# One loop for TensorE over both layers, a bias table with its heads side by side, and products that nobody reads

## The reference

```
x = x + attention(group_norm(x))          # twice

def attention(x):                          # windows of 8 x 8 tokens, shifted by 4; 16 heads of 16
    q, k, v = xw @ Wq.T, xw @ Wk.T, xw @ Wv.T + bv
    logits = norm(q) @ norm(k).T * exp(min(logit_scale, log 100))
    tab = relu(table @ cpb_w1.T + cpb_b1) @ cpb_w2.T       # 225 positions x 16 heads
    logits += 16 * sigmoid(tab[relative position])          # 64 x 64 x 16
    logits = where(mask, -inf, logits)
    z = softmax(logits) @ v @ Wo.T + bo
```

## Time and profile before

| | |
|---|---|
| median of three runs | 826.88 us (823.43 to 829.28) |
| the profiled execution | 830.89 us, its span 828.7 us |
| mean granted clock of TensorE | 0.933 of full speed |
| busy: TensorE, its weight loads | 750.0 us, 670.4 us |
| busy: VectorE, ScalarE, GpSimd | 530.2, 519.3, 556.1 us |

### The profile page before, as it was taken

One profiled execution on the slowest core, in us unless ns is written; L12 is line 12 of the kernel. 1 busy time (PEld: TensorE's weight loads), 2 busy tenths in 40 slices (PEclk: granted clock), 3 DMA queues, 4 the chain that ended last, 5 costly groups with the idle time before them and its releaser, 6 DMA issues.

```text
span 828.7 us, 38879 instructions
## 1 busy us (share of the span) xinstructions
PE 750.0 (91%) x15514; PEld 670.4 (81%) x15514; DVE 530.2 (64%) x1184; ACT 519.3 (63%) x978; POOL 556.1 (67%) x917
## 2 busy tenths in 40 slices
PE   2569199999999999998999999999999999999995
PEld 1468188888888898887988888888888888888884
DVE  3246057777777777777675566777777777776442
ACT  3355147777777777776575566777676677666550
POOL 3456057777777778776576567777777777777560
PEclk9868669999999999999798899999999999999895
DMA  3620654000000000000000000000000000000000
GB/s 105 84 65 3 70 167 127 0 0 0 0 0 0 0 0 0 0 1 2 2 3 2 15 16 26 26 25 25 13 25 25 25 25 25 25 13 27 28 28 30
DMA packets 17438, 21.91 MB, mean 26 GB/s; under 512 B 7353, under 2 KB 8674, under 8 KB 17378
## 3 DMA queue, kind: packets, MB, share of 16 engines
q1 hardware_dynamic: 16834, 20.30, 9.5%
q10 hardware_dynamic: 544, 0.79, 0.3%
HBM read 12.66 MB, written 8.42 MB: 25 GB/s over the span
## 4 chain that ended last, share of the span: by engine, by line
PE 83%; issue 4%; DVE 4%; DMA 3%; SPq 2%; POOL 1%; ACT 1%; DVEq 1%; POOLq 0%; ACTq 0%
PE ps_qk L379 21%; PE ps_mix L493 16%; PE ps_qk L505 13%; PE ps_mix L413 8%; PE ps_score L403 6%; PE ps_score L466 6%; PE ps_mix L418 4%; PE ps_mix L391 3%; PE ps_mix L483 3%; DVE x_out L766 2%; SPq L306 2%; DMA x_all<-in_x 1%; DMA bias_rev<-table_scratch 1%; PE ps_score L430 1%; DVE exp_bias L258 1%
## 5 line engine op out<-in xcount | busy, mean ns | idle before, releaser
L938 POOL TENSOR_TENSOR probs<-probs,exp_bias 128x512 f32<-128x512 f32 x256 | 321.1, 1290 | 15.1 <-DVE exp_bias L258 7.8
L379 PE MATMUL ps_qk<-w_qk,xn 128*128 128x512 f32 x768 | 204.3, 417 | 0.8 <-POOL xn L886 0.6
L636 ACT ACTIVATE probs<-ps_score,lower 128x512 f32<-128x512 f32 x256 | 155.1, 689 | 74.0 <-PE ps_score L466 74.0
L379 PEld LDWEIGHTS ps_qk<-w_qk,xn 128*128 128x128 f32 x768 | 147.3, 199 | 32.5 <-POOL xn L886 0.7
L493 PE MATMUL ps_mix<-v_ones,probs 64*64 64x17 f32 x8064 | 140.8, 212 | 7.0 <-issue 7.0
L493 PEld LDWEIGHTS ps_mix<-v_ones,probs 64*64 64x64 f32 x8064 | 133.5, 141 | 8.1 <-issue 6.3
L568 ACT ACTIVATE squares<-ps_qk 128x512 f32<-128x512 f32 x128 | 76.5, 598 | 87.7 <-PE ps_qk L379 87.6
L505 PE MATMUL ps_qk<-w_v,xn 128*128 128x256 f32 x768 | 117.2, 307 | 6.4 <-DVE unit L755 6.4
L730 DVE TENSOR_REDUCE sums_sq<-squares 128x32 f32<-128x512 f32 x128 | 86.2, 677 | 52.6 <-ACT squares L568 52.6
L755 DVE SCALAR_TENSOR_TENSOR unit<-root,ps_qk 128x512 f32<-128x512 f32 x128 | 82.3, 684 | 58.1 <-POOL root L920 58.1
L505 PEld LDWEIGHTS ps_qk<-w_v,xn 128*128 128x128 f32 x768 | 103.6, 207 | 10.6 <-issue 6.7
(11 more groups left out here) (78 smaller groups left out, 977.3 us busy)
## 6 DMA issues: line engine op xcount, KB each, us to landing
x_all<-in_x SPq DMA_DIRECT2D x32, 256.0 KB, 2.9
out<-x_out SPq DMA_DIRECT2D x32, 256.0 KB, 2.1
bias_rev<-table_scratch SPq DMA_DIRECT2D x32, 56.5 KB
probs<-in_L_matrices ACTq DMA_DIRECT2D x1, 512.0 KB, 5.0
w_o_in<-in_L_matrices SPq DMA_DIRECT2D x4, 128.0 KB
x_out<-in_L_matrices SPq DMA_DIRECT2D x1, 512.0 KB, 4.5
probs<-in_L_matrices ACTq DMA_DIRECT2D x1, 256.0 KB, 5.3
allowed<-in_L_matrices SPq DMA_DIRECT2D x1, 256.0 KB, 5.1
```

Source lines behind the costliest of these rows:

```text
L379: last = nc.tensor.matmul(ps_qk[:, e, :], xn[:, px, t.parity, c, e * P:(e + 1) * P], w_qk[:, pw, t.layer, c, :], start=(c == 0 and i == 0) ...
L636: nc.scalar.activation(probs[:, t.parity, r, :, :, :, :].rearrange("p e c a n -> p (e c a n)"), ps_score[:, r, :], ACT.Exp, bias=lower[:, ...
L938: nc.gpsimd.tensor_tensor(pr, pr, exp_bias[:, t.layer, r, :, :, :, :].rearrange("p e c a n -> p (e c a n)"), ALU.mult).then_inc(weighted, 1)
```

## The change

- TensorE has one loop, rounds 4 to 61; the other engines keep two (SP's first ends at round 25). `run` takes the loops as an argument. For that, `w_qk`, `w_v` and `w_o` hold one layer only; layer 1's weights are split over them in rounds 31, 32 and 34, once their last reader is through. Their raw copies have buffers of their own instead of borrowed ones.
- The table has positions on partitions (113 and 112 of them) and heads along the columns, for both layers at once, in round -2 and -1. A position's 16 heads lie side by side in memory, and what one key position needs is one piece of 113 x 16 values. `spread_bias` is two transfers a layer; layer 1's goes out in round 2.
- Images are loaded six jobs ahead instead of four; the constants are loaded second.
- TensorE's first instruction is the product of group means of job 0; the table comes behind it. On ScalarE the table's work stands behind the roots of job 0. GpSimd does `mean_squares` last in the rounds before 0.
- `mask_bias` is VectorE's alone, four operations on 128 partitions: at the end of round 0 for layer 0, one each at the end of rounds 28 to 31 for layer 1.
- `sum_out_bias` does both layers in round 1.
- `keep_busy`: products of 128 x 128 x 128 whose result nobody reads, 12 in round -1, 16 in round 0 behind the q/k product, and 8 and 4 in each of rounds 65 and 66.

```diff
-        def run(engine, iteration, exact):
+        def run(engine, iteration, exact, loops):
...
-            for layer in range(LAYERS):
-                first, last, rest = ((4, 28, IMAGES + 4), (IMAGES + 4, 60, JOBS + 4))[layer]
+            some(-WARM, loops[0][0])
+            for n, (first, last) in enumerate(loops):
+                rest = loops[n + 1][0] if n + 1 < len(loops) else JOBS + 4
                 with engine.Fori((first + JOBS * exact) // 2, (last + JOBS * exact) // 2) as half:
...
             def spread_bias(l):
-                for w in range(2):
-                    for row in range(WIN):
-                        src = bass.AP(table_scratch.tensor, table_scratch.offset + l * HEADS * REL * REL + row * REL,
-                                      [[1, WIN], [REL * REL, HEADS], [1, RUN]])
...
+                for w in range(2):
+                    src = bass.AP(table_scratch.tensor, table_scratch.offset + l * HEADS * REL * REL,
+                                  [[REL * HEADS, WIN], [HEADS, WIN], [1, RUN * HEADS]])
+                    dst = bias_rev[w * N:(w + 1) * N, 0:RUN, :].rearrange("p k h -> p (k h)")
+                    sp.dma_start(dst, src).then_inc(bias_in, 16)
...
                 if j == -WARM and not base.exact:
+                    keep_table()
                     spread_bias(0)
-                if j == 1 - WARM and not base.exact:
+                    load_x(Job(2, 0, 0, 0))
+                    load_x(Job(2, 1, 0, 0))
                     load_out(0)
-                if j == 3 and not base.exact:
+                    load_out(1)
+                if j >= 0:
+                    load_x(job(j, base, PREFETCH))
+                if j == 2 and not base.exact:
                     load_qkv(1)
-                    load_out(1)
+                    sp.wait_ge(bias_ready, 2 * CC)
                     spread_bias(1)
-                if j >= 0:
-                    load_x(job(j, base, 4))
...
-                        last = nc.tensor.matmul(ps_qk[:, e, :], xn[:, px, t.parity, c, e * P:(e + 1) * P], w_qk[:, pw, t.layer, c, :],
+                        last = nc.tensor.matmul(ps_qk[:, e, :], xn[:, px, t.parity, c, e * P:(e + 1) * P], w_qk[:, pw, c, :],
...
+            def keep_busy(cols, n):
+                for _ in range(n):
+                    nc.tensor.matmul(cols, group_mean[:, :], group_mean[:, :], start=True, stop=True, skip_group_check=True)
...
+                if j in (JOBS + 1, JOBS + 2) and not base.exact:
+                    keep_busy(ps_qk[:, 0, 0:P], 8)
...
+                if j == -1 and not base.exact:
+                    keep_busy(ps_score[:, 3, 0:P], 12)
                 project_qk(now, 1)
+                if j == 0 and not base.exact:
+                    keep_busy(ps_score[:, 3, 0:P], 16)
                 turn_back(oldest)
+                if j in (JOBS + 1, JOBS + 2) and not base.exact:
+                    keep_busy(ps_qk[:, 0, 0:P], 4)
...
-            both_passes(pe, iteration)
+            both_passes(pe, iteration, ((4, JOBS - 2),))
...
+                if j == IMAGES - 1:
+                    act.wait_ge(qk_done, now.count(2, 2))
+                    round_weights(1, 0)
+                if j == IMAGES:
+                    act.wait_ge(v_done, before.count(1, 1))
+                    round_weights(1, 1)
+                if j == IMAGES + 2:
+                    act.wait_ge(z_done, oldest.count(1, 1))
+                    round_weights(1, 2)
...
+                if j == IMAGES:
+                    split_weights(1, base.exact, 1)
                 make_unit(base, now, 1)
+                if j == IMAGES - 1:
+                    split_weights(1, base.exact, 0)
+                if j == IMAGES + 2:
+                    split_weights(1, base.exact, 2)
                 make_unit(base, now, 0)
                 divide(older)
+                if j == 0 and not base.exact:
+                    for e in range(2):
+                        for c in range(CC):
+                            mask_bias(0, e, c)
+                if IMAGES - 4 <= j < IMAGES and not base.exact:
+                    mask_bias(1, *divmod(j - IMAGES + 4, CC))
```

300 lines of the change are left out of this document (148 added, 152 removed).

## The result

| | before | after |
|---|---|---|
| median of the runs | 826.07 us (823.43 to 829.28, 4 runs) | 775.02 us (773.81 to 776.61, 4 runs) |
| the profiled execution | 830.89 us, span 828.7 | 774.51 us, span 772.6 |
| mean granted clock | 0.933 | 0.98 |

The ratio is 0.9382, 95% interval 0.9343 to 0.9421: 51 us faster. Forecast were 760 us, range 749 to 773, so the time lies 2 us outside it.

A forecast was written before the change was run, and what follows sets the result against it. TensorE's own work, plus stretches where it waits and then runs at 1.2 instead of 2.4 GHz, was taken as the bound. Span 828.7 - 44 (start) - 21 (middle) - 2 (end) = 761.7 us; median 760, range 749 to 773.

The forecast's parts named there:

- 15.97 - 5.55 = 10.4 us: Round 1: VectorE's 5.55 us wait for the fifth image goes, so the round falls from 15.97 to 10.4 us.
- The unread products of the start: Rounds -1 and 0: twelve and sixteen unread products fill TensorE's gaps at full clock; round 0 takes 10.5 instead of 12.1 us.
- Rounds 2 to 5: TensorE's 19.87 us hole, behind VectorE's wait for x, goes whole; the four rounds take 45.7 instead of 77.7 us.
- The middle: Rounds 28 to 38: masks and splits fit VectorE's rounds, one TensorE loop removes instruction-fetch holes; 21 us less, bounds 10 and 22.
- slack of 2.6: Around round 28: a round swallows 2.6 us of extra VectorE work (5.65 - 3.02) before TensorE notices.
- rival 1: Rounds 28 to 32: VectorE is late after all, with one or two falls of the clock; +10 us, 770; 12%.
- rival 4: TensorE's loop: its body is fetched again each pass, 2.0 us a round over 58 rounds; +116, 876 us; 2%.
- The end: Round 60 to the span's end: loop exit 1 us less, unread products in the last two rounds 1 us less; 2 together.
- stick out by 0.5: Last rounds: the first eight unread products, 1.9 us at full speed, outlast their 1.4 us gap by 0.5 us.
- Rival 2: Start and end: unread products run at 1.2 GHz and outlast their gaps; +9 to +12 us, 770; 14%.
- From profile to median: Whole kernel: the profiled execution lies 4.0 us over the median, so 763.9 with a profile becomes 760 us.
- Rival 3: Rounds 32 to 37: holes come with the layer, not TensorE's fetches, so 12 of 22 us stay; 772 us; 4%.

## Why the prediction missed

**The sum.** The span came out at 772.6 against 761.7, 10.9 us more: start +8.2, rounds 6 to 27 +1.2 (round 6 takes 11.7), middle -1.2, rounds 38 to 59 +0.5, end +2.0, the rest is rounding. The step from profile to median adds 4.5 (3.9 down in the forecast, 0.5 up in fact), what lies around the span takes 0.3: 15 us in all.

**The start: the step that failed is "15.97 - 5.55 = 10.4 us" for round 1.** It took 17.1. I had the table "read back by 22, an estimate from the rates of the rows" and the masks at 2.5 us behind it. The read ended at 27.5 and took 11.0 us from its first issue, 9.1 in the best form tried; the masks took 3.99, between my bounds and near the upper one, 4.4. (The same columns took 2.51 before. They now read the table with the heads innermost, so at a stride; that this is why wasn't tried.) Both lie ahead of round 1's work on VectorE, TensorE waits 4.90 us and goes on at half clock. That this is the cause of the long round is shown by the masks moved one round on: round 1 at 11.05 us. (It doesn't follow that the time would have fallen by as much: there rounds 2 and 4 gave the gain back.) The sign that I had named for this came too: round 6 starts at 91.8, after 90, and VectorE waited for the bias transfers.

The from which the rate came show many transfers at once, 196 GB/s; this read alone moved 0.93 MB in 9.97 us, 93 GB/s. The Trainium skill (DMA: Bandwidth & Descriptors, section Anatomy of one DMA) fits a transfer that GpSimd issues as 2.0 us and its bytes at 436 GB/s. If that held for these two, which SP issues, they would take some 4 us, an estimate from the page. The measurement of 9.97 decides. The write of the 64-B pieces (450 by the shapes of its two transfers, not 449) took 3.85 us and was over at 16.5, against the 16 that I had; whether the Trainium skill's rule on short pieces, which I weighed there, has a part in that no run shows.

And I had costed the product of both layers' bias of v, moved into round 1, at nothing; it takes 3.57 us at half clock, 2.39 in the run without unread products, where the clock was up for most of it.

**The unread products of the start** worked as priced (round 0 at 9.3 us instead of 10.5), but what they win has no way to the end. Twelve and sixteen in gaps were a gain for round 0 and none for round 2: the three kernels without them start round 2 earlier, by 1.1 to 2.0 us. I had priced round 1 as if it followed round 0 and nothing else.

**Rounds 2 to 5: right in the main, 2.9 us short.** The hole of the earlier trace rows went whole, as said: VectorE waits for an image once, 4.1 us for the first. The order of loads alone, in the kernel before, is worth 2.5% or 20 us (interval 1.8 to 3.3%). What I had under "filling TensorE's instruction buffer", with the split of the weights 1.5 us together, took more: rounds 4 and 5 have holes of 1.01 and 0.38 us with the low clock behind each, 13.7 and 12.9 us.

**The middle: the size came out (21 forecast, 22.2 measured), the reasons only in part.** The masks and splits cost TensorE one wait, in round 32:

```profile
386.23 0.73 PE L419 MATMUL ps_mix<-mixed,w_o 128*128 128x256 f32 x4 [0.77 <-DVE mixed L787]
```

Round 31's split had taken 2.00 us and its mask 1.59, together 3.6 where I had 1.84 to 2.3, and so over the slack of 2.6; VectorE was busy without a pause from there to `mixed`. Round 32 took 12.0 us, the others from 28 to 31 10.9 to 11.0. That is about the 1 us that I had left; a fall of the clock, as in rival 1, did not come of it.

Apart from the first pass, q8 is silent in the loop over 29 passes, so rival 4 did not come. The Trainium skill (Runtime: NRT & Kernel Launch, section Instruction fetch mechanics) has a taken branch fetch its target if that lies outside the two pages in sight, and says that kernels prefer full unrolling. The trace agrees with neither here: the loop's first pass took four blocks, its 28 jumps back fetched nothing, and the written-out rounds are those that wait for instructions.

But the loop's own share is 5 us in the run that tried it, not 12. In rounds 32 to 37 of before the holes make 3.7 us, and the clock was at 1.2 GHz for 17 us behind three of them; at half speed that costs up to 8.5, enough for the rest of the 12. With two loops in the kernel after, the holes make 2.9 us and it fell behind one; in the kernel with images six ahead they make 2.5 us, it fell behind none, and the rounds take 11.5 to 11.7 us. What the loop saves so depends on how often the clock falls, and that changes from execution to execution of one kernel too. (Two readings were off: the page's line of the clock has one 7 and two 8s in the middle, not two 7s, and the stretch of the earlier trace rows holds some ten passes of the loop, not 12.)

**The end: 0 instead of 2 us.** In the profiled execution "stick out by 0.5" was the wrong term: the first eight products took 3.60 us at 1.2 GHz, behind a hole of 1.33 us, instead of 1.9. The last mix but one ran in 2.05 us as forecast. But in the repeat of the same kernel that hole was 0.71 us long, the eight took 2.05 us, and round 60 to the end took 76.8 us, where I had forecast 77.0. So the 2 us are one execution's holes and its clock, and no fault of the products is shown: with them and without them the end from round 63 takes 40.6 us where no such hole comes ahead, and 42.6 and 42.4 us where holes do. Against my 1 us of gain they are worth nothing. Rival 2 had 4 to 8 us more at the end; the end was as long as before in one execution and 2.2 us shorter in the other. At the start it did not come either.

**From profile to median.** 4.0 us were carried over from the kernel before. In the fourteen groups of runs since, the profiled execution stood from 2.8 below to 2.2 above its median (after 0.5 below, in the repeat 2.2 below). Single runs of the kernel before went from 815.4 to 830.4 us. So I take the 4.0 for chance; they should have widened the range instead of moving the forecast.

Rival 3 fell too: in the loop of one piece the rounds 32 to 37 have no holes that end at nothing, stores or not, and with two loops they stand in rounds 28 to 32, ahead of the stores.

What stays open: why a hole at one place takes 0.43 us in one run and 0.97 in another, behind which of them the clock falls, and why the table's read uses half of the engines.

## What to carry to other kernels

A fill of work that nobody reads helps only if the next wait doesn't stand at a fixed time: look what the following round waits for first, here a table's way through memory, and price that with its own transfer, not with the rate of many at once. A stretch that holds both waits and a fallen clock must be split into the two before one edit is given all of it; of the 22 us in the middle the loop took 5 in the run that tried it alone. Price one edit at the end of a kernel by two executions at least: here the same kernel differed by 2.9 us from round 63 on, as much as the edit seemed to bring. And the distance between one profiled execution and the median belongs in the range.

## What the runs showed of the hardware

- TensorE ran a loop whose body is two rounds from 90.7 to 722.3 us with no block of instructions fetched. A 16-KB block of code that runs for the first time can cost it a hole, 0.3 to 3.0 us in the kernels after, and the hole ends 1.2 to 1.6 us after the block has landed (86 of 89 in all the traces). A shift of the code by 28 products moved the holes to other products.
- The granted clock fell to 1.2 GHz behind some holes of 0.4 to 1 us and stayed full behind others of the same size, in the same kernel: in round 62 it stayed full behind 0.78 us in after and fell behind 0.77 in its repeat, in round 5 it fell behind 0.38 us and stayed full behind 0.40.
- A read of 128 pieces of 7232 B that overlap in memory took 9.97 us with no other load beside it; most of the time eight were under way, 0.50 us each. In pieces of 3616 and 1808 B, beside the same images, the time from SP's first issue fell from 11.0 to 9.5 and 9.1.
- A mask of 128 x 512 took VectorE 1.0 us at the start, where GpSimd was quiet, and 1.85 at 346.83 us, beside GpSimd's weighing (343.99 to 349.78).
